# Low-rank adapters: from all eight computed and masked to each batch item's own, picked by index

## The reference, cut to what matters

```
x = x + attention(conditioned(x, i))            # 16 heads, causal, T = 32
gate = x @ Wg + (x @ Ag[i]) @ Bg[i]             # Wg 256x1024, Ag[i] 256x16, Bg[i] 16x1024
up   = x @ Wu + (x @ Au[i]) @ Bu[i]
h    = silu(gate) * up
y    = h @ Wd + (h @ Ad[i]) @ Bd[i]             # Wd 1024x256, Ad[i] 1024x16, Bd[i] 16x256
u    = fwht(silu(y @ W1.T) * (y @ W3.T))        # Walsh-Hadamard transform over 1024
x = x + u @ W2.T
```

## Time and profile before

| | |
|---|---|
| median of 3 runs | 227.52 us (227.52 to 227.6) |
| the profiled execution | 227.53 us, its span 225.7 us, TensorE clock 0.999 |
| PE busy | 98% of the span, 1485 matmul records |
| PEld, POOL, ACT, DVE busy | 79%, 53%, 44%, 38% |
| DMA | 13.02 MB, mean 58 GB/s |

### The profile page before, as it was taken

The page is one execution under the profiler, slowest core; times in us unless marked ns, Lnnn a source line. Parts: engine busy times, 40 slices in busy tenths (PEclk is TensorE's granted clock), DMA queues, the critical chain, the costliest instruction groups (busy, mean ns, idle before and its releaser), DMA issues.

```text
span 225.7 us, 3708 instructions
## 1 busy us (share of the span) xinstructions
PE 221.0 (98%) x1485; PEld 178.4 (79%) x1485; DVE 85.0 (38%) x142; ACT 100.2 (44%) x169; POOL 120.8 (53%) x93
## 2 busy tenths in 40 slices
PE   7999998999999999999999999999999999999995
PEld 2577786878788888888888888888888888888894
DVE  4998999898345431210032000203222222220211
ACT  2389799896754325740564000304355555440000
POOL 1029677547786208999999800270266677443000
PEclk9999999999999999999999999999999999999999
DMA  6955500004025001230020000031101100000211
GB/s 180 416 215 180 141 3 4 3 3 139 3 70 159 4 3 15 80 93 26 0 69 24 0 3 0 0 98 42 46 9 47 41 3 0 1 0 0 82 60 46
DMA packets 5345, 13.02 MB, mean 58 GB/s; under 512 B 720, under 2 KB 1360, under 8 KB 5072
## 3 DMA queue, kind: packets, MB, share of 16 engines
q1 hardware_dynamic: 4896, 11.72, 16.7%
q10 hardware_dynamic: 432, 1.07, 1.4%
HBM read 11.73 MB, written 1.05 MB: 57 GB/s over the span
## 4 chain that ended last, share of the span: by engine, by line
PE 86%; ACT 6%; DVE 3%; DMA 1%; issue 1%; POOL 1%; DVEq 0%; ACTq 0%
PE bank L388 27%; PE bank L392 27%; PE bank L390 27%; ACT k_x L682 4%; PE bank L407 2%; PE bank L490 1%; DMA index_i<-index 1%; PE bank L414 1%; ACT k_x L704 1%; DVE k_x L941 1%; ACT prob L698 1%; DVE cond_sel L890 1%; DVE k_x L884 1%; ACT v_tok L692 0%; POOL prob L1170 0%
## 5 line engine op out<-in xcount | busy, mean ns | idle before, releaser
L1183 POOL TENSOR_TENSOR h_lo<-tmp_b,h_hi 128x512 fp32r<-128x512 f32 x32 | 41.1, 1303 | 32.2 <-ACT h_hi L731 32.2
L388 PE MATMUL bank<-act_hi,w_hi 128*128 128x512 f32 x152 | 52.8, 392 | 0.1
L392 PE MATMUL bank<-act_hi,w_lo 128*128 128x512 f32 x152 | 52.4, 389 | 0.0
L390 PE MATMUL bank<-act_lo,w_hi 128*128 128x512 f32 x152 | 52.3, 389 | 0.0
L1029 DVE TENSOR_TENSOR tmp_b<-bank,tmp_a 128x512 f32<-128x512 f32 x32 | 21.1, 688 | 73.6 <-PE bank L392 41.1
L1145 POOL TENSOR_TENSOR w_lo<-raw,w_hi 128x512 fp32r<-128x512 f32 (+3 forms) x22 | 35.9, 1642 | 10.2 <-ACT w_hi L666 10.2
L388 PEld LDWEIGHTS bank<-act_hi,w_hi 128*128 128x128 f32 x152 | 28.5, 188 | 6.9 <-issue 1.1
L392 PEld LDWEIGHTS bank<-act_hi,w_lo 128*128 128x128 f32 x152 | 28.5, 188 | 6.0
L390 PEld LDWEIGHTS bank<-act_lo,w_hi 128*128 128x128 f32 x152 | 28.5, 188 | 5.8
L731 ACT ACTIVATE h_hi<-tmp_b 128x512 fp32r<-128x512 f32 x32 | 19.8, 633 | 27.0 <-DVE tmp_b L1029 27.0
L388 PE MATMUL bank<-h_hi,w_hi 128*128 128x512 f32 (+1 forms) x88 | 27.3, 370 | 0.0
(11 more groups left out here) (88 smaller groups left out, 255.4 us busy)
## 6 DMA issues: line engine op xcount, KB each, us to landing
raw<-w_stream SPq DMA_DIRECT2D x13, 256.0 KB, 2.7
raw<-w_stream SPq DMA_DIRECT2D x8, 384.0 KB, 3.2
raw<-w_stream SPq DMA_DIRECT2D x3, 512.0 KB, 3.7
k_x<-x_slots ACTq DMA_DIRECT2D x2, 512.0 KB, 6.6
tmp_b<-w_t SPq DMA_DIRECT2D x1, 1024.0 KB, 8.9
resid<-x_feat SPq DMA_DIRECT2D x1, 1024.0 KB, 10.6
out_feat<-tmp_b SPq DMA_DIRECT2D x3, 256.0 KB, 2.1
out_feat<-tmp_b SPq DMA_DIRECT2D x2, 128.0 KB, 1.8
```

Of the source, the lines that this page charges most:

```text
L388: pe.matmul(ps[:, :], w[0], x_hi, start=start, stop=False)
L390: pe.matmul(ps[:, :], w[0], x_lo, start=False, stop=False)
L392: last.append(pe.matmul(ps[:, :], w[1], x_hi, start=False, stop=stop))
L1183: pool.tensor_tensor(lo, tmp_b[:, n % 4, :], f32(hi), ALU.subtract).then_inc(prod_split, 1)
```

## The change: what it does

- No adapter is computed for an item that does not use it, and there is no mask. `adapter_values` loads indices into registers of SP, DVE or POOL. POOL (`gather_in`, eight calls of four copies) and DVE (`gather_down`, eight calls of four copies) copy each item's 16 columns of A on the chip, from a raw copy of all adapters, at an address from the register. The rows of B come by DMAs from DRAM at such an address, 16 rows each: 32 for Bg/Bu (`load_b_own`), 32 for Bd (`load_b_down`).
- The adapter matmuls are plain fp32, small, and placed in parts of the array: A products with 32 columns (two items) and 64 tokens; B products with 64 rows (four items) and 128 tokens. DVE spreads the result to slots (`own_slots`) in place of the mask and the split.
- h @ Ad is done tile by tile (`down_adapters_in`) beside the gate/up work, from `tmp_b`.
- The halves' order changes (ALONE 6 instead of 5, then half by half); gate and up are finished in pairs of m.
- W2 is loaded late into `tmp_a`, and fold, butterflies (now on DVE) and its rests run behind gate/up.
- The side bias of the conditioning is one matmul over 40 rows and not two. The early part is reordered, key before query, half 1's conditioning later; 7 keep-warm matmuls instead of 3.
- Weight batches are all 512 columns in a ring of six places.

```
-W_Q, W_K, W_V, W_OUT, W_A, W_GU = 0, 1, 2, 3, 4, 5
+W_Q, W_K, W_V, W_OUT, W_GU = 0, 1, 2, 3, 4
-KEEP_WARM = 3
-ALONE = 5
+ALONE = 6
+KEEP_WARM = 7
...
# SP, after the first loads
+            first_half, second_half = adapters(0, BH), adapters(BH, BH)
...
+            wait_full(sp, "s", 0, TILES_S - 1)
+            load_b_own(0, 0, first_half, 0, BH)
+            wait_full(sp, "s", 1, TILES_S - 1)
+            for m in range(1, 4):
+                load_weights(W_GU + m)
+            wait_full(sp, "z", 0, 0)
+            load_weights(W_GU + 4)
+            load_b_own(1, 0, second_half, 0, BH // 2)
+            load_weights(W_GU + 5)
+            wait_full(sp, "y", 1, TILES_Y - 1)
+            sp.wait_ge(turned, HALVES * TILES_S)
+            sp.dma_start(a_down_raw..., w_stream[:, PACKED_AT[P_AD]:...])
+            wait_full(sp, "z", 1, 0)
+            load_b_own(2, 0, second_half, BH // 2, BH // 2)
+            for n in range(W_GU + 6, W_D + 3):
                 load_weights(n)
+            load_b_down(0, BH)
+            load_weights(W_D + 3)
+            load_b_down(BH, B)
+            wait_read(sp, "up", 1, HC - 1)
+            sp.dma_start(tmp_a[:, :, :], w2_t...).then_inc(w2_loaded, 16)
...
# PE: adapters_in(s), c, a, q, h, e = 2 each: 32 matmuls
+    last = pe.matmul(ps[64 * h + 32 * e:64 * h + 32 * e + 32, (2 * a + q) * 2 * T:(2 * a + q + 1) * 2 * T],
+                     a_in[:, s, a * DC + c, b:b + 2, :]..., resid[:, c, at:at + 2 * T], ...)
# PE: adapters_out, one call for a pair of (s, m): 16 matmuls
+                for step in range(4):
+                    for h in range(2):
+                        if step >= 2:
+                            pe.wait_ge(half_added[1 - h], 2 * n + step - 1)
+                    for q in range(2):
+                        for h in range(2):
+                            name, s, m = tiles[(step + 2 * h) % 4]
+                            rows_ = slice(64 * h, 64 * h + 64)
+                            at = (2 * q + h) * P
+                            ins = pe.matmul(tile(name, s, m)[:, at:at + P], weight(name, s, m, rows_, q),
+                                            slots(name, s, rows_, q)..., start=False, stop=True, ...)
# PE: down_adapters_in, for each (s, m) of a pair: q, h, e = 2 each: 8 matmuls
+                                ins = pe.matmul(ps[64 * h + 32 * e:64 * h + 32 * e + 32, ...],
+                                                a_down[:, m, s * BH + b:s * BH + b + 2, :]...,
+                                                tmp_b[:, n % 4, b * T:(b + 2) * T], ...)
# PE: the order from the second half's attention on
+            adapters_in(0)
+            gate_up(0, 0)
+            gate_up(1, 0)
+            gate_up_adapters((0, 0), (0, 1))
+            gate_up(2, 0)
             values(1, 0)
+            gate_up(3, 0)
             values(1, 1)
             project(1, 0, 0, 1)
...
+            for s, m in GU_ORDER[10::2]:
+                for k in (m, m + 1):
+                    gate_up(k, s)
+                down_adapters_in(*GU_ORDER[GU_ORDER.index((s, m)) - 2:GU_ORDER.index((s, m))])
+                gate_up_adapters((s, m), (s, m + 1))
...
+            down(0, 0, 2)
+            down_adapters_in(*GU_ORDER[-2:])
+            down(0, 2, HC)
...
+            down(1, 0, 2)
+            for j in range(4):
+                fold(j)
+            down(1, 2, HC // 2)
...
+            adapters_out(len(GU_ORDER) // 2, [("d0", 0, 0), ("d1", 0, 0), ("d0", 1, 0), ("d1", 1, 0)], ...)
+            for s, ins in enumerate(down(1, HC // 2, HC)):
+                full(ins, "d1", s, 0)
...
# POOL: early order
-            pool.wait_ge(fbias_made, 4)
-            fold_raw_lo(0)
-            weights_lo(W_OUT)
-            fold_raw_lo(1, 2, 3)
-            weights_lo(W_A)
-            weights_lo(W_GU)
-            normalised(0, 0, 1, 2)
+            pool.wait_ge(fbias_made, 2)
+            gather_in(0, 0)
...     seven calls in all
+            gather_in(1, 2)
+            normalised(0, 0, 1)
+            spread_first(0, 0, 1)
+            normalised(0, 2, 3)
+            spread_first(0, 2, 3)
             weights_lo(W_OUT)
             weights_lo(W_GU)
# POOL gather_in (DVE gather_down is of the same form, from a_down_raw to a_down)
+                adapter = adapter_values(mybir.EngineType.Pool, b0, 4)
+                pool.wait_ge(a_in_raw_loaded, 16)
+                for b in range(4):
+                    last = pool.tensor_copy(a_in[:, s, :, 4 * i + b, :],
+                                            a_in_raw[:, :, bass.DynSlice(adapter[b], 1), :]...)
```

More of the change, by code:

```diff
@@ L62 @@
 MASKED = -1e30
+LO_ROW = 32
+BIAS_ROWS = LO_ROW + N
 C_CAUSAL = 0
@@ L339, in f32, with adapter_values @@
             return ap.bitcast(F32)
+        def adapter_values(engine, b0, n):
+            _, values = nc.values_load_multi_w_load_instructions(
+                index_i[0:1, NG + b0:NG + b0 + n], engines=[engine], min_val=0, max_val=N - 1,
+                skip_runtime_bounds_check_because="an adapter's index lies in 0 to N - 1, as the reference's gather needs")
+            return values
         block = ctx.enter_context(nc.Block())
@@ L523, in gate_up @@
                         pe.wait_ge(x1_split, DC * ss[-1] + c + 1)
[L524 to L534 removed]
+                        both(tiles, unit(w, a * DC + c), rows(act_hi, act_lo, c, ss), c == 0, c == DC - 1)
@@ L594, in _ @@
             gate_up(0, 1)
[L595 removed]
+            down_adapters_in((0, 2), (0, 3))
             gate_up(1, 1)
[L597 removed]
+            gate_up_adapters((1, 0), (1, 1))
             gate_up(2, 1)
[L599 to L606 removed]
@@ L609, in _ @@
-            down = {}
-            for name, n in (("d0", W_D0), ("zd", W_AD), ("d1", W_D1)):
-                w = weights(n)
-                tiles = down[name] = [claim(name, s, 0) for s in range(HALVES)]
-                for k in range(HC):
-                    pe.wait_ge(prod_split, SPLIT_COUNT["up", 1, k])
-                    last = both(tiles, unit(w, k), h_rows(k), k == 0, name == "zd" and k == HC - 1)
-                if name == "zd":
-                    for s in range(HALVES):
-                        full(last[s], name, s, 0)
@@ L619, in _ @@
-            w = weights(W_BD)
-            pe.wait_ge(prod_split, SPLIT_COUNT["zd", 1, 0])
-            for s in range(HALVES):
-                for m, name in enumerate(("d0", "d1")):
-                    last = both([down[name][s]], unit(w, m), rows(aux_hi, aux_lo, 0, [s]), False, True)
-                    full(last[0], name, s, 0)
+            down_adapters_in((0, 4), (0, 5))
+            gate_up(3, 1)
+            down_adapters_in((1, 0), (1, 1))
+            gate_up_adapters((1, 2), (1, 3))
@@ new lines, in _, with down @@
+            for s, m in GU_ORDER[10::2]:
[3 more added lines that the diff above has]
+                gate_up_adapters((s, m), (s, m + 1))
+            def down(m, k0, k1):
+                tiles = [tile(f"d{m}", s, 0) for s in range(HALVES)]
+                for k in range(k0, k1):
+                    w = weights(W_D + 2 * m + k // 4)
+                    pe.wait_ge(prod_split, ORDINAL["up", 1, k] + 1)
+                    last = both(tiles, unit(w, k % 4), h_rows(k), k == 0, k == HC - 1)
+                return last
@@ L835, in _ @@
[L835 to L845 removed]
+            hidden_hi(0, 5)
@@ new lines, in slot_free, with butterflies @@
+                if 4 <= n < len(GU_ORDER) + 3:
+                    dve.wait_ge(zd_read, n - 3)
+                elif n == len(GU_ORDER) + 3:
+                    wait_full(dve, "zd", 0, 0)
+            def butterflies(stage, t):
+                if stage == 0 and t == 0:
+                    for j in range(4):
+                        wait_read(dve, "fold", 0, j)
+                if stage:
+                    dve.wait_ge(butterfly, 2 * stage)
+                w = D << stage
+                a, b = (w2_fold[:, (stage + x) % 2].rearrange("p (u t w) -> p t u w", t=2, w=w) for x in range(2))
+                dve.tensor_tensor(b[:, t], a[:, 0], a[:, 1], ALU.subtract if t else ALU.add)\
+                    .then_inc(butterfly, 1)
@@ new lines, in own_slots @@
+            def own_slots(name, s, out, even):
+                wait_full(dve, name, s, 0)
+                ps = tile(name, s, 0)[:, 0:4 * 2 * T].rearrange("p (x f t) -> p x f t", x=4, t=T)
+                for e in range(2):
+                    last = dve.tensor_tensor(out[:, :, e].rearrange("p x (f t) -> p x f t", t=T), ps,
+                                             four[:, 2 * e:2 * e + 2].unsqueeze(1).unsqueeze(3)
+                                             .to_broadcast([P, 4, 2, T]), ALU.mult)
+                    if e == 0:
+                        last.then_inc(even, 1)
+                free(last, name, s, 0)
@@ new lines, in outputs_lo @@
+            def outputs_lo(m):
+                for s in range(HALVES):
+                    dve.wait_ge(y2_hi_made, HALVES * m + s + 1)
```

(8 more changed lines are left out.)

739 lines of the change are left out of this document (405 added, 334 removed), and 24 rows, old and new, of the table EARLY_BANKS.

## The result

The changed kernel takes 218.14 us (median of four runs, 217.52 to 219.22) against 227.55 us: a ratio of 0.959, 95% interval 0.955 to 0.963. The forecast was 217.5. Run again beside the first experiments, it took 217.98 us (six runs, 215.94 to 219.92), a ratio of 0.957 (0.953 to 0.960). Ratios are taken over the runs within 1.5% of a kernel's fastest, medians over all. The kernel before repeats within 0.1 us here; the changed one spreads over 1.7 us, and over 4 us when run again, and that spread turned out to be the clue to what the prediction had not seen.

A forecast was written before the change was run, and what follows sets the result against it. The prediction took PE, busy in 98% of the span, as the bound: 225.7 - 40.8 + 27.0 = 211.9 us, plus 2.3 early, 1.0 W2 and 0.5 attention, span 215.7, plus 1.8 around it: 217.5 us, range 210 to 226.

The forecast's parts named there:

- The part removed and PE's net: On PE: 180 adapter matmuls at 0.227 us go, 40.8 us; 27.0 us of small ones come; net 211.9 us.
- late waits: Behind the early part: 1.0 us stall for W2 before the last fold, 0.5 us for half 1's attention.
- adapters_out: On PE: nine calls of 32 records at 60 ns, 2.2 us each with shape changes, 19.8 us (16.4 to 35.4).
- down_adapters_in: On PE: 32 records for each of 8 pairs at 17 ns, 4.8 us with shape changes (4.3 to 16).
- shape changes: On PE: switching matmul shape costs 0.10 us at each side, three changes in a pair.
- the full drain: On PE: alternative price for some 28 shape changes, 0.06 us more each, 1.7 us in all.
- The second rival: In adapters_out on PE: row halves run one after the other, 3.9 us a call, 233 us, slower than before; 8%.
- The first rival: Everything overlaps: adapters_out at 1.8 us a call, 22.9 us added, no stall, 209.6 us; 15%.
- The early part: Before gate_up(0, 0): gathers at 1.8 us a call put `normalised` at 30.3 and gate_up at 47.5, +2.3 us.
- the case in which the term is 0: Early part: gather calls take 1 us, PE's own work ends there, and nothing is added to the span.
- b_own(0) is 16 of them ... hidden: SP's queue: 16 DMA issues, 7 to 11 us, begun near 25 and needed near 53, cost nothing.
- The queues further on: Later SP, DVE and POOL work is hidden, except 1.0 us for W2 (0 to 1.9) and 0.5 for half 1's attention.

The follow-up runs named there:

- kernel 10: Changed kernel with its first 16 indexed B loads issued in two parts, eight from about 16 us and eight from about 25.4 us: 214.56 us.
- kernel 4: Changed kernel with each of the 28 early copies of A columns by a register made twice, the second into unused space: 223.59 us.
- kernel 2: Changed kernel with B rows packed contiguously, one run of 8 KB per row in place of 16 pieces of 512 bytes: 217.90 us.

## Why the prediction was right, point by point

- **The part removed and PE's net** (211.9 us of span): 1.0 too low. From the start of gate_up(0, 0) to the end the prediction has 215.7 - 47.5 - 1.5 of late waits = 166.7; the profiles have 167.7 in the changed kernel (from 47.98) and in kernel 10 (from 45.02). Summed from PE's starts in the changed kernel, the nine calls of adapters_out are 17.9 us and not 17.3, down_adapters_in 4.7 and not 4.3, the shape changes 3.4 and not 3.0 (by the full drain that the prediction weighed they would be 4.7); adapters_in and the moved `values` call give back 0.2 each. So the part added was 28.0 and not 27.0. No run takes the change apart; that the gain is PE's work less, 40.8 out and 28.0 in, rests on this sum and on PE's busy time, 12.0 us less.
- **adapters_out** at 60 ns a record (of 57 to 68), 1.92 a call: 62 ns, 1.98. The overlap of row halves, read from 64x32 calls, holds for 128-column weight loads too: each still takes 188 ns, and one starts every 62 ns, so its duration is not its price. The waits between halves were put at nothing; together with whatever else is in the 0.58 us of a call, they may not be. **down_adapters_in** 17 ns: 18. **adapters_in** 1.2: 1.03. **Shape changes** 0.10 at each side: 0.09 to 0.11.
- **The second rival** (halves one after the other, 3.9 us a call, 233 us, slower than before): made real it is 4.09 a call and 236.9, a ratio of 1.039. Its mechanism was right, and it is not what the chip does here. Its sum has a slip: 9 x 3.9 is set against the 2.2 that holds 0.28 for shape changes, which the serial call has too; with them it is 2.5 us more, 235.5. The first rival's 16.4 leaves them out in the same way.
- **The early part**: the sum came out (47.5 predicted, 47.98 measured) for the wrong reason. The step "I take 0.5 [for a register load] ... 1.8 a call ... `normalised` starts at 30.3" failed: a call costs 0.88, `normalised` starts at 24.60. By the prediction's own remark that is the case in which the term is 0, and kernel 10 shows 45.02 where 45.2 had been worked out (though by its own chain the term is 0 from 1.5 us a call down, not from 1). The chain behind `normalised` was too short, 9.1 us to the second `values` where the changed kernel has 11.6 and kernel 4 has 11.3, and so was the part from there to gate_up: 8.1, and 9.0 in kernel 10, with the DVE wait of 0.81. The Trainium skill (DMA: Bandwidth & Descriptors, Latency and other measured facts) has the floor of some 600 ns for a tensor_load; here GpSimd's take 0.31 to 0.33 us, the first 0.53, one for the four registers of a call, partly beside the copies, and the measurement decides. That the gathers' chain reaches PE was read rightly: kernel 4, at 1.49 a call, makes PE wait 2.32 us.
- **What filled the place**: PE's stop of 2.06 to 2.40 us and the half clock behind it: gate_up(0, 0) starts 2.96 us later in the changed kernel's profile than in kernel 10's. The step "b_own(0) is 16 of them ... hidden" failed. It counted SP's issue time and the landing against the reader, and both are hidden; that the transfers are in the way of PE's own instructions was not in it.
- **The queues further on**: 1.0 for W2 and 0.5 for half 1's attention came to 0. W2's DMA took 5.0 us from issue to landing, not 6 to 9.
- So: PE's term 1.0 too low, the early part +2.8 in place of +2.3 by another mechanism, the late waits 1.5 too high. The errors cancel: the profile's span is 215.7, the very number of the forecast, and that is luck. The 0.6 us between 217.5 and 218.14 is not among them: the profiled execution is the fastest of the four (217.52), and the slowest, 219.22, is the one with the lowest mean clock, 0.984.

## What to carry to other kernels

A gap on the busiest engine that the profile gives to "issue", in the middle of a loop of small instructions, is worth a look at what the DMA engines carry at that moment: many tiny matmuls use up instructions fast (64 records in 1.09 us here), and the next block can be late. The cheapest test is to move the transfer, not to reshape it. And a total that comes out right is no proof of its terms: the spread of the changed kernel, 1.7 us over its first four runs against 0.08 for the one before, said so before any experiment.

## What the runs showed of the hardware

- GpSimd copies 128x64 fp32 values at a register's index in 0.18 us from one start to the next; the load of four registers takes 0.31 to 0.33 us (0.53 the first).
- Instructions reach PE in 16 KB blocks over the same DMA engines as data. A block's fetch took 0.90 to 1.05 us (the first five of the kernel before, where later ones took up to 1.44) and 1.6 us beside the indexed loads at 150 GB/s, and started up to 3.0 us late there (up to 5 with all 16 loads earliest). The Trainium skill (Runtime: NRT & Kernel Launch, Instruction fetch mechanics) has the blocks of 16 KiB and says that fetching is mostly hidden; the trace agrees on the blocks and, at 17 ns a record with data in flight, not on the hiding.
- Loads of 128 KB into 16 partitions move at 139 to 164 GB/s together, in pieces of 512 bytes as in runs of 8 KB; SP issues one with an indexed source in 0.57 us (16 in 9.13). The plain loads at the start reach 393 in one slice of the page.
- A stop of 2 us and more was followed in most profiles by a stretch at the 1.2 GHz level, 3.4 us long in the profile after, where a call of 1.11 us took 1.88; kernel 2's profile has a stop of 2.40 and no such stretch. In the three kernels whose profile shows a stop of 0.53, 0.60 or 1.08 us, the mean clock was 0.998 or more in all fifteen runs.
